# A Fourier-layer image tower on one core: the inverse x step moved whole behind the centre taps, in a hand-written order of matmuls

## The chip, the core and the metric

The kernel runs on one core of a Trainium2 chip. The metric is the device time of one execution in microseconds (us). Three runs of the kernel before took 1215.12, 1220.45 and 1225.88 us, median 1220.45.

A core has five engines with an instruction stream each: TensorE (PE; its weight loads are listed as PEld), VectorE (DVE), ScalarE (ACT), GpSimd (POOL) and SyncE (SP). Here SP and POOL issue the DMAs. Each engine runs its own stream in order; where one needs another's result it waits on a counting semaphore.

## The reference, cut to what matters

```python
h = concatenate([grid, x], -1) @ P_w + P_b              # 32 images, 64x64, 32 channels
for i in range(4):                                      # the four layers
    h_ft = rfft2(h)
    out_modes = einsum('bixy,ioxy->boxy', h_ft[:, :, :16, :16], spec_w[i])   # complex
    spec = irfft2(out_modes, s=(64, 64))
    conv = conv2d(h, conv_w[i], 3x3, 'SAME') + conv_b[i]
    h = leaky(spec + conv)
h = leaky(h @ Q1_w + Q1_b) @ Q2_w + Q2_b                # one channel: 32 x 64 x 64
h = h + attention(layernorm(h))                         # rows of an image are the tokens
h = h + mixture(layernorm(h))                           # causal attention, gates, small MLP
```

Only 16 x 16 Fourier modes are kept, so both transforms are matrix products with constant matrices. All data is fp32.

## The kernel before, in words

**Units.** The 32 images are worked in 16 pairs (`PAIRS`), four layers one after the other; T = 16 l + p counts pairs over all layers, `LAST` is p = 15. One pair's plane is 128 partitions by four *units* u of 512 values. Each unit has an accumulator of one PSUM bank, `acc[u]`.

**What is summed in an accumulator.** In layer 0 the first layer's convolution is folded into one product with `xcol` (`convolve_first`, one product per unit). In layers 1 to 3 the 3x3 convolution reads `halo`, a shifted copy of the plane in SBUF, in three kinds of products: `convolve_centre` (four 128x512 products, one per unit), `convolve_rows(T, v)` (v = 0 works on units 0 and 2, v = 1 on units 1 and 3; 16 products each) and `convolve_columns(T, v)` (8 each, same units). Onto the same accumulators `spectral(T, part)` adds the last step of the inverse transform, the inverse x step: 64 products of 64x64 in four parts of 16. ACT then reads the four accumulators (`evict`, one ACTIVATE each, bias and leaky) into `x_now`.

An fp32 product is recorded as two matmuls and two weight loads. In the profile's counts a pair has therefore 8 centre, 64 row, 32 column and 128 spectral matmuls.

**The transforms around it.** DVE transposes `x_now` (`turn_x`, two pieces, tile `xt`), PE does the rows of the forward transform (`rows_forward`, 16 matmuls by the profile's count), DVE transposes (`turn_rows`, tile `ft`), PE does the columns (`columns_forward`, 64), ACT copies the modes into `spec` (`spectrum`). At the layer's end `mix` multiplies all modes by the layer's weights `wspec` (256 matmuls in four quarters), and DVE turns each quarter (`turn_modes`, tile `zt`). For each pair `columns_back` (32) starts the inverse, DVE transposes (`turn_back`, tile `vt`), and `spectral` ends it. One part of `wspec` has to be negated on DVE before `mix` (`negate`). Between layers a pair's plane goes to HBM by a POOL DMA (`store`) and comes back as `halo` by 11 SP DMAs (`load_halo`).

**What sets the order.** Everything is written out by hand. For PE a pair is one function: `first_pair` (layer 0), `pair` (layers 1 and 2), `last_pair` (layer 3, with the head of pair p-1 and pieces of the later attention, `fronts`, between); `boundary` is the first pair of layers 1 to 3. DVE's loop over T is: `turn_rows(T+1)`, `turn_back(T+1)`, `turn_x(T+2)`, and for p = 8 `negate(l+1)`. ACT's loop over T is four `evict`, then `spectrum(T-1)`. PSUM is full: four accumulators, two banks for the forward transform, two for the inverse. So a unit's next centre product waits until ACT has read that accumulator (`s_x`), and `rows_forward(n)` waits for `turn_x(n)`, which waits for all four evictions of pair n-2.

## Time and profile before

| | us |
|---|---|
| median of 3 runs | 1220.45 |
| the profiled execution | 1218.4 |
| its span, first to last instruction | 1216.6 |
| PE busy | 1069.0 (88%) |
| DVE busy | 612.0 (50%) |
| ACT busy | 456.5 (38%) |
| mean granted TensorE clock | 0.963 of full |

A span is what the hardware profiler saw between the first and the last instruction; the execution's own time is 1.8 us more. Idle before an instruction is named with what released it; "issue" means that the engine waited for nothing that the profile shows. The rows on which the prediction rests stand two sections below.

### The profile page before, as it was taken

What the parts mean: (1) busy time and instruction counts of PE and PEld (TensorE: products, weight loads), DVE (VectorE), ACT (ScalarE), POOL (GpSimd) and SP (SyncE); (2) the same over time, 40 slices, a digit from 0 to 9 for tenths busy, and PEclk for the clock granted to TensorE, in tenths of its full rate; (3) what the DMA queues carried; (4) which work ended last, traced back from release to release, by engine and by line L of the source; (5) the groups of instructions that cost most, each with busy time, mean ns of one, the idle gap of its engine ahead of it and who ended that gap; (6) DMA issues with size and microseconds to landing.
All of it is one profiled execution on the core that took longest, in us unless ns stands there. A gap on an engine that the chain in (4) does not pass through costs nothing.

```text
span 1216.6 us, 47905 instructions
## 1 busy us (share of the span) xinstructions
PE 1069.0 (88%) x22416; PEld 565.3 (46%) x22416; DVE 612.0 (50%) x548; ACT 456.5 (38%) x889; POOL 83.7 (7%) x154
## 2 busy tenths in 40 slices
PE   4688888789989999889999899888999999899965
PEld 2445545454444444554444444533343444366722
DVE  3777787545555754455556554510221423277743
ACT  1245445313333332223333333223344443566523
POOL 2000000000000000000000000001212112110000
PEclk9899989899999999999999999999999999899986
DMA  9364445666776766686776767478545544000000
GB/s 312 143 209 135 133 135 165 200 218 192 210 223 201 225 210 195 197 283 213 217 212 208 219 205 212 134 182 201 139 115 141 145 121 108 5 6 1 2 1 17
DMA packets 50805, 194.25 MB, mean 160 GB/s; under 512 B 14928, under 2 KB 15696, under 8 KB 41040
## 3 DMA queue, kind: packets, MB, share of 16 engines
q1 hardware_dynamic: 40624, 138.23, 41.2%
q0 software_dynamic: 9984, 52.97, 12.0%
q8 instruction: 176, 2.88, 1.0%
q14 instruction: 21, 0.17, 0.0%
HBM read 138.19 MB, written 52.95 MB: 157 GB/s over the span
## 4 chain that ended last, share of the span: by engine, by line
PE 74%; DVE 8%; issue 8%; ACT 4%; DMA 1%; SPq 0%; DVEq 0%; ACTq 0%
PE psum L593 14%; PE psum L607 13%; PE psum L636 11%; PE psum L620 6%; PE psum L566 5%; PE psum L514 4%; PE psum L501 4%; PE psum L551 3%; ACT x_now L1017 3%; PE psum L654 3%; DVE xt L1195 2%; PE psum L838 2%; PE psum L578 1%; DMA halo<-activations 1%; PE psum L662 1%
## 5 line engine op out<-in xcount | busy, mean ns | idle before, releaser
L1017 ACT ACTIVATE x_now<-psum,conv_bias 128x512 f32<-128x512 f32 x256 | 157.4, 689 | 514.3 <-PE psum L636 497.2
L1195 DVE STREAM_TRANSPOSE xt<-x_now 128x1024 f32<-128x1024 f32 x100 | 204.5, 2082 | 116.4 <-ACT x_now L1017 110.5
L1225 DVE STREAM_TRANSPOSE vt<-psum 128x1024 f32<-128x1024 f32 x64 | 125.4, 1960 | 197.5 <-PE psum L566 197.5
L593 PE MATMUL psum<-halo,conv 128*128 128x512 f32 x384 | 184.8, 623 | 2.2 <-ACT x_now L1017 1.8
L607 PE MATMUL psum<-halo,conv 64*32 64x512 f32 x3072 | 177.7, 592 | 0.4 <-issue 0.4
L1202 DVE STREAM_TRANSPOSE ft<-psum 128x1024 f32<-128x1024 f32 x50 | 100.4, 2009 | 151.6 <-PE psum L501 151.5
L636 PE MATMUL psum<-dft,vt 64*64 64x64 f32 x8192 | 147.9, 222 | 27.7 <-issue 26.9
L636 PEld LDWEIGHTS psum<-dft,vt 64*64 64x64 f32 x8192 | 133.4, 136 | 72.6 <-issue 59.5
L325 ACT ACTIVATE spec<-psum 32x128 f32<-32x128 f32 x372 | 142.7, 384 | 40.3 <-PE psum L514 36.3
L593 PEld LDWEIGHTS psum<-halo,conv 128*128 128x128 f32 x384 | 71.3, 197 | 87.3 <-issue 61.2
L607 PEld LDWEIGHTS psum<-halo,conv 64*32 64x32 f32 x3072 | 53.4, 106 | 116.0 <-issue 115.8
L514 PE MATMUL psum<-dft,ft 128*32 128x64 f32 x3200 | 65.0, 232 | 35.8 <-issue 27.7
L620 PE MATMUL psum<-halo,conv 64*32 64x512 f32 x1536 | 93.6, 591 | 0.0
L566 PE MATMUL psum<-zt,dft 64*32 64x256 f32 x2048 | 82.0, 379 | 2.7 <-DVE vt L1225 1.4
L445 POOL DMA_DIRECT2D activations<-x_now x48 | 25.7, 535 | 726.5 <-ACT x_now L1017 726.5
L514 PEld LDWEIGHTS psum<-dft,ft 128*32 128x32 f32 x3200 | 53.4, 117 | 46.8 <-issue 29.2
L566 PEld LDWEIGHTS psum<-zt,dft 64*32 64x32 f32 x2048 | 50.7, 106 | 47.9 <-issue 37.4
L501 PE MATMUL psum<-xt,dft 64*32 64x512 f32 x800 | 55.6, 612 | 17.5 <-DVE xt L1195 17.5
L578 PE MATMUL psum<-xcol,conv 96*128 96x512 f32 x128 | 64.2, 647 | 0.0
L1024 ACT ACTIVATE xt<-psum,q1b 128x512 f32<-128x512 f32 x64 | 40.4, 683 | 44.2 <-PE psum L654 44.0
L620 PEld LDWEIGHTS psum<-halo,conv 64*32 64x32 f32 x1536 | 29.6, 106 | 54.7 <-issue 50.2
L452 POOL DMA_DIRECT2D tower_out<-ft x64 | 31.8, 503 | 245.6 <-ACT ft L1031 229.8
(150 smaller groups left out, 783.0 us busy)
## 6 DMA issues: line engine op xcount, KB each, us to landing
activations<-x_now POOLq DMA_DIRECT2D x48, 1056.0 KB, 7.2
halo<-activations SPq DMA_DIRECT2D x384, 132.0 KB, 4.7
halo<-activations SPq DMA_DIRECT2D x48, 528.0 KB, 5.7
halo<-activations SPq DMA_DIRECT2D x96, 264.0 KB, 6.3
wspec<-in_spec SPq DMA_DIRECT2D x16, 1024.0 KB, 10.1
xcol<-in_xcol SPq DMA_DIRECT2D x16, 384.0 KB, 4.4
x_now<-in_ser SPq DMA_DIRECT2D x2, 1056.0 KB, 6.9
spec<-in_onehot SPq DMA_DIRECT2D x1, 2048.0 KB, 17.7
```

Source lines behind the costliest of these rows:

```text
L325: return copy(spec[g:g + 32, 64 * qh:64 * qh + 64, ql, 2 * p:2 * p + 2].rearrange("p (y x) b -> p y b x", x=MODES), columned(X + 2)[32 * q ...
L501: z = mm(rowed[g:g + 32, f, :], ex[64 * f:64 * f + 64, :], xt[64 * f:64 * f + 64, at:at + 16, :], start=True, stop=True)
L514: z = mm(columned(n)[g:g + 32, 64 * kyb:64 * kyb + 64], ft[:, k0, :], ey[:, ri, :], start=(ri == 0), stop=(ri == 1))
L566: z = mm(backed[g:g + 32, cg, 256 * ri:256 * ri + 256], iy[64 * cg:64 * cg + 64, m, 32 * h:32 * h + 32], zt[64 * cg:64 * cg + 64, :, 2 * p ...
L593: mm(acc[u], centre[l - 1][:, u // 2, :], window(T, 0, None, u, 0, 0), start=True, stop=False, skip_group_check=True)
L607: z = mm(acc[u][g:g + 32, :], weight[64 * f:64 * f + 64, s, :], window(T, 0, f, u, di, dj), start=False, stop=False, skip_group_check=True)
L620: mm(acc[u][g:g + 32, :], edge_x[l - 1][64 * f:64 * f + 64, h, r, :], window(T, 1, f, u, 0, -1 if s == 0 else 1), start=False, stop=False, ...
L636: z = mm(acc[u][64 * s:64 * s + 64, at:at + 64], vt[64 * il:64 * il + 64, k, 4 * u + ih].rearrange("p r o -> p (r o)"), ix[64 * il:64 * il ...
L1017: copy(x_now[:, k, 16 * u:16 * u + 16, 0:G], acc[u].rearrange("p (i j) -> p i j", j=G), ACT.Prelu, bias=conv_bias[:, l:l + 1], alpha=SLOPE ...
L1195: vec.transpose(xt[:, 32 * m:32 * m + 32, :], x_now[:, n % 2, :, 0:G].rearrange("p (i m) j -> p m j i", m=2)[:, m]).then_inc(s_xt, 1)
L1202: vec.transpose(ft[:].rearrange("p k c -> p c k"), rowed.rearrange("p a b -> p (a b)").rearrange("p (i c) -> p c i", c=C)).then_inc(s_ft, 1)
L1225: vec.transpose(vt[:, k].rearrange("p h r o -> p (h r) o").rearrange("p y o -> p o y"), backed.rearrange("p a b -> p (a b)").rearrange("p ...
```

## The change

1. In layers 1 to 3 `spectral` moves from the end of a pair to right behind the four centre products, all four parts; the row and column products follow, and the column products now end a unit. Units 0 and 2 are then complete before 1 and 3, so centres and evictions go in the order 0, 2, 1, 3 (`units`, `evicted`). In `pair` the forward rows stand between the two halves of the row products. The first pair of a layer keeps its spectral step at the end.
2. In layer 0 a pair was: convolution, `rows_forward(T+1)`, `columns_back(T+1)`, `spectral(T)`, `columns_forward(T+1)`. It is now: two convolution products, `columns_forward(T)`, the other two, `spectral(T)`, `rows_forward(T+1)`, `columns_back(T+1)`. ACT's `spectrum` of layer 0 moves ahead of the evictions.
3. `negate` is cut from 4 instructions into 8 (`NEGATED`), the four quarters of `mix` wait for two each. In layer 0's own start it stands behind the copies of the modes; for the next layer one piece stands in each of the pairs 8 to 15.
4. The 4 MB of the next layer's weights, which SP issued in one go behind `mix`, go in four pieces with the pairs 2 to 5. The two masks of layer 3 (2 MB each), issued behind the halo of pair 3, go in four pieces with the pairs 3 to 6.
5. At the start PE waits for `dft` alone (`s_dft`), and the folding of weights stands behind the first forward rows. ACT's `head_read` stands behind all four evictions.

The places in PE's stream, first a pair of layer 1 (T = 17) and the head of the next, before. L593 is `convolve_centre`, L607 the row products, L501 `rows_forward`, L620 the column products, L566 `columns_back`, L636 `spectral`, L514 `columns_forward`; here a row counts fp32 products, half of the profile's matmuls:

```order
L593 MATMUL psum<-halo,conv 128x512 x4
L607 MATMUL psum<-halo,conv 32x512 x32
L501 MATMUL psum<-xt,dft 32x512 x8
L620 MATMUL psum<-halo,conv 32x512 x16
L566 MATMUL psum<-zt,dft 32x256 x16
L636 MATMUL psum<-dft,vt 64x64 x64
L514 MATMUL psum<-dft,ft 32x64 x32
```

And a pair of layer 1 (T = 18) with the change, where all these lines are 12 to 15 higher (L606 centre, L651 spectral, L620 rows, L513 forward rows, L633 columns, L578 back, L526 forward columns):

```order
L606 MATMUL psum<-halo,conv 128x512 x4
L651 MATMUL psum<-dft,vt 64x64 x64
L620 MATMUL psum<-halo,conv 32x512 x16
L513 MATMUL psum<-xt,dft 32x512 x8
L620 MATMUL psum<-halo,conv 32x512 x16
L633 MATMUL psum<-halo,conv 32x512 x16
L578 MATMUL psum<-zt,dft 32x256 x16
L526 MATMUL psum<-dft,ft 32x64 x32
```

The three rows of small products (16, 64 and 32) stood next to each other and are now in two places, 64 behind the centres and 48 at the end.

A pair of layer 0 on PE before (L578 is `convolve_first`):

```order
L578 MATMUL psum<-xcol,conv 128x512 x4
L501 MATMUL psum<-xt,dft 32x512 x8
L566 MATMUL psum<-zt,dft 32x256 x16
L636 MATMUL psum<-dft,vt 64x64 x64
L514 MATMUL psum<-dft,ft 32x64 x32
```

and with the change (L591 is `convolve_first`):

```order
L591 MATMUL psum<-xcol,conv 128x512 x2
L526 MATMUL psum<-dft,ft 32x64 x32
L591 MATMUL psum<-xcol,conv 128x512 x2
L651 MATMUL psum<-dft,vt 64x64 x64
L513 MATMUL psum<-xt,dft 32x512 x8
L578 MATMUL psum<-zt,dft 32x256 x16
```

`rows_forward` stood ahead of the pair's own `spectral` and stands behind it now.

DVE ahead of layer 0's `mix` before (L1212 is `negate`, L1315 the copies of the modes):

```order
L1195 STREAM_TRANSPOSE xt<-x_now 128x1024 x2
L1202 STREAM_TRANSPOSE ft<-psum 128x32x32
L1212 TENSOR_SCALAR wspec<-wspec 32x64x32 x4
L1315 COPY spec<-psum 64x4x64 x16
L1218 STREAM_TRANSPOSE zt<-psum 128x1024 x4
```

and with the change (L1240, L1342):

```order
L1223 STREAM_TRANSPOSE xt<-x_now 128x1024 x2
L1230 STREAM_TRANSPOSE ft<-psum 128x32x32
L1342 COPY spec<-psum 64x4x64 x16
L1240 TENSOR_SCALAR wspec<-wspec 32x8x4x32 x8
L1246 STREAM_TRANSPOSE zt<-psum 128x1024 x4
```

The negation, now in 8 pieces of half the size, stands behind the copies.

The diff, cut to its core:

```diff
-        NEGATED = 4
+        NEGATED = 8
+        def units(T):
+            return (0, 1, 2, 3) if T < PAIRS else (0, 2, 1, 3)
+        def evicted(T, u):
+            return 4 * T + units(T).index(u) + 1
...
-                    load_weights(l + 1)
                 for p in range(2, PAIRS):
                     T = l * PAIRS + p
+                    if l < NL - 1 and p < 6:
+                        load_weights(l + 1, p - 2)
...
-                    if l == NL - 1 and p == 3:
+                    if l == NL - 1 and 3 <= p < 7:
+                        b = slice(8 * (p - 3), 8 * (p - 3) + 8)
                         sp.wait_ge(s_mix, 4 * NL)
-                        sp.dma_start(lq[64:128]..., onehot_d).then_inc(t_mask, 16)
-                        sp.dma_start(kr[64:128]..., causal_d).then_inc(t_mask, 16)
+                        sp.dma_start(lq[64:128, b]..., onehot_d[:, b]).then_inc(t_mask, 16)
+                        sp.dma_start(kr[64:128, b]..., causal_d[:, b]).then_inc(t_mask, 16)
...
             def mix(l):
-                pe.wait_ge(s_neg, NEGATED * (l + 1))
...
                 for c in range(4):
+                    pe.wait_ge(s_neg, NEGATED * l + 2 * c + 2)
...
             def first_pair(p):
                 T = p
-                if p > 0:
-                    for u in range(4):
-                        convolve_first(T, u)
-                    rows_forward(T + 1)
-                if p < LAST:
+                for i in range(4):
+                    if p > 0:
+                        convolve_first(T, i)
+                    if p > 1 and i == 1:
+                        columns_forward(T)
+                if p == 0:
                     columns_back(T + 1)
                 for part in range(4):
                     spectral(T, part)
                 if p > 0:
-                    columns_forward(T + 1)
+                    rows_forward(T + 1)
+                if 0 < p < LAST:
+                    columns_back(T + 1)
             def pair(l, p):
...
+                for u in units(T):
+                    convolve_centre(T, u)
+                for part in range(4):
+                    spectral(T, part)
+                convolve_rows(T, 0)
+                rows_forward(T + 1)
+                convolve_rows(T, 1)
+                convolve_columns(T, 0)
+                convolve_columns(T, 1)
                 if p < LAST:
                     columns_back(T + 1)
-                for part in range(4):
-                    spectral(T, part)
-                if p > 0:
-                    columns_forward(T + 1)
+                columns_forward(T + 1)
...
-            pe.wait_ge(s_const, 16 * 4)
-            fold_weights()
+            pe.wait_ge(s_dft, 16)
             rows_forward(0)
+            pe.wait_ge(s_const, 16 * 3)
+            fold_weights()
...
-                evict(T, 0)
+                if l == 0 and p > 1:
+                    spectrum(T - 2)
+                for u in units(T):
+                    evict(T, u)
                 if last and p > 0:
                     head_read(p - 1)
-                for u in range(1, 4):
-                    evict(T, u)
...
-            negate(0)
             for n in range(1, 2 * SERIES, 2):
...                                                          # the copies of the modes
+            negate(0, *range(NEGATED))
...
-                        if p == PAIRS // 2:
-                            negate(l + 1)
+                        if p >= PAIRS - NEGATED:
+                            negate(l + 1, p - (PAIRS - NEGATED))
```

`last_pair` and `boundary` change in the same manner: `spectral` right behind the centres, and in layer 1's `boundary` the `columns_forward(T)` that layer 0 no longer has done.

## Rows read from the trace of the kernel before

**Rows 1.** The page: busy times, DMA queues (packets, MB, share), the chain by engine.
```profile
PE 1069.0 (88%) x22416; PEld 565.3 (46%) x22416; DVE 612.0 (50%) x548; ACT 456.5 (38%) x889; POOL 83.7 (7%) x154
...
q8 instruction: 176, 2.88, 1.0%
...
PE 74%; DVE 8%; issue 8%; ACT 4%; DMA 1%; SPq 0%; DVEq 0%; ACTq 0%
```

**Rows 2.** Windows of PE: from:to, length, busy (matmuls), granted clock, DMA share, GB/s.
```profile
74.50:148.40 73.90, 63.59 (x1751) 1.00 0.45 143
148.40:173.40 25.00, 21.05 (x515) 0.86 0.38 121
173.40:228.00 54.60, 45.13 (x1221) 0.97 0.67 202
228.00:260.40 32.40, 26.00 (x703) 0.95 0.37 134
260.40:281.00 20.60, 15.18 (x289) 0.91 0.75 232
281.00:496.80 215.80, 201.52 (x4798) 0.98 0.71 214
541.30:756.60 215.30, 200.17 (x4784) 0.99 0.72 214
801.70:843.50 41.80, 35.43 (x616) 0.92 0.94 208
843.50:859.60 16.10, 15.75 (x320) 0.98 0.55 139
843.50:1050.20 206.70, 205.47 (x3814) 1.00 0.47 121
```

**Rows 3.** Timeline of layer 0: start, us, what; in brackets idle before and releaser.
```profile
128.21 3.70 PE L578 MATMUL psum<-xcol,conv 96*128 96x512 f32 x8
...
129.29 4.08 DVE L1195 STREAM_TRANSPOSE xt<-x_now 128x1024 f32<-128x1024 f32 x2 [1.21 <-ACT x_now L1017]
...
133.42 1.09 PE L501 MATMUL psum<-xt,dft 64*32 64x512 f32 x16 [1.51 <-DVE xt L1195]
...
134.62 1.99 DVE L1202 STREAM_TRANSPOSE ft<-psum 128x1024 f32<-128x1024 f32 x1 [1.25 <-PE psum L501]
...
135.51 2.35 PE L636 MATMUL psum<-dft,vt 64*64 64x64 f32 x128
136.47 1.95 DVE L1225 STREAM_TRANSPOSE vt<-psum 128x1024 f32<-128x1024 f32 x1
137.40 2.42 ACT L1017 ACTIVATE x_now<-psum,conv_bias 128x512 f32<-128x512 f32 x4 [5.15 <-PE psum L636]
```

**Rows 4.** Timeline of layer 0, middle: the negation of the next weights.
```profile
154.98 4.97 DVE L1212 TENSOR_SCALAR wspec<-wspec 32x2048 f32<-32x2048 f32 x4
```

**Rows 5.** Timeline of the start, before the first pair.
```profile
9.07 2.02 PE L521 MATMUL psum<-fold_w,fold_p 128*96 128x128 f32 x8 [9.07 <-DMA proj<-in_proj]
...
30.52 4.97 DVE L1212 TENSOR_SCALAR wspec<-wspec 32x2048 f32<-32x2048 f32 x4 [7.66 <-DMA wspec<-in_spec]
...
36.76 7.76 PE L534 MATMUL psum<-series,proj 128*32 128x256 f32 x88 [7.61 <-DVE spec L1315]
...
46.49 7.68 PE L551 MATMUL psum<-spec,wspec 128*64 128x64 f32 x256 [1.97 <-ACT spec L1083]
...
55.52 1.13 PE L566 MATMUL psum<-zt,dft 64*32 64x256 f32 x32 [1.34 <-DVE zt L1218]
```

**Rows 6.** Windows of PE in layer 1: a pair without idle; one stall to the next.
```profile
314.40:328.35 13.95, 13.95 (x346) 1.00 0.63 203
359.44:376.07 16.63, 15.00 (x382) 1.00 0.67 202
```

**Rows 7.** Timeline of PE at the second of these stalls.
```profile
371.18 2.36 PE L636 MATMUL psum<-dft,vt 64*64 64x64 f32 x128
...
376.08 0.41 PE L514 MATMUL psum<-dft,ft 128*32 128x64 f32 x11 [1.63 <-issue]
```

More of the change, by code:

```diff
@@ L763, in last_pair @@
                 if p > 0:
-                    for u in range(4):
+                    for u in units(T):
                         convolve_centre(T, u)
+                    for part in range(4):
+                        spectral(T, part)
                     fronts(p, 0)
@@ L777, in last_pair @@
                     columns_back(T + 1)
-                for part in range(4):
-                    spectral(T, part)
-                    if p > 0 and part == 1:
-                        head_out(p - 1)
+                if p == 0:
+                    for part in range(4):
+                        spectral(T, part)
+                else:
+                    head_out(p - 1)
                 fronts(p, 2)
@@ L786, in boundary @@
                 T = l * PAIRS
-                for u in range(4):
+                for i, u in enumerate(units(T - 1)):
                     convolve_centre(T, u)
+                    if l == 1 and i == 1:
+                        columns_forward(T)
                 rows_forward(T + 1)
```

69 lines of the change are left out of this document (36 added, 33 removed).

## The prediction, made before the change was run

> **What bounds the kernel now.** I read the page first. PE is busy for 88% of the span and carries 74% of the chain that ended last, but 8% of that chain is "issue": PE waits and nothing shows why [rows 1]. Then I cut PE's time at each pair's first eviction and looked at windows [rows 2]; the cuts are evictions of T = 1, 8, 10, 15, 16, 17, 31, then 33, 47, 49, 51, 52 and 63.
>
> *Layer 0* takes (73.90 + 25.00 + 54.60) / 14 = 10.96 us a pair, and PE is idle in 10 of 74 us [rows 2]. The timeline shows the loop [rows 3]: `turn_x` 4.08 us on DVE ends at 133.37, the forward rows start at 133.42, `columns_back` and `spectral` follow, the eviction starts at 137.40, takes 2.42, and the next `turn_x` starts behind it. From `turn_x` at 129.29 that is 4.08 + 0.05 + 3.98 + 2.42 = 10.5 us. The eviction of pair T waits for the forward rows of T+1 only because they stand ahead of `spectral(T)` on PE.
>
> *Layers 1 and 2* take 215.80 / 14 and 215.30 / 14, or 15.4 us a pair, while a pair without idle takes 13.95 [rows 2, 6]. 1.43 us a pair are lost. The loss has a period. From one unexplained stall to the next PE issues 382 matmuls [rows 6], three times 127. A matmul comes with a weight load, and the instruction queue moved 2.88 MB in 176 packets for 2 x 22416 such records [rows 1], 255 for a packet. So PE stops at the edges of instruction blocks that have not arrived. The block behind the second stall starts at 376.08. The one before it began 127 matmuls earlier, 54 into the burst of 128 at 371.18 [rows 7], so at 372.0. The time from a block's begin to the next block's readiness, L, was 4.0 us there. A block that runs shorter than L ends in a stall. `columns_back`, `spectral` and `columns_forward` are 224 matmuls in some 4.2 us (128 of them in 2.36 with their tail [rows 7]), so a block that lies in them runs about 2 us. Averaged over where a block's edge may fall in the pair's 344 matmuls (2.7 edges a pair), L = 3.9 gives 1.57 us a pair, L = 3.5 gives 1.16. The measured 1.43 is L of about 3.8.
>
> The Trainium skill ("Runtime: NRT & Kernel Launch", Instruction fetch mechanics) confirms blocks of 256 instructions, but says that PE buffers 2048 of them and that crossing an edge is mostly hidden. By that rule the stalls have another cause; its time stands among the rivals. The measured spacing of 382 and the 4.0 us speak against the second half of the rule.
>
> *Layer 3* runs without idle from 843.50 (205.47 busy of 206.70), but its two pairs at 801.70 take 41.80 us at a DMA share of 0.94, against 16.1 for the next pair [rows 2]: the two masks, 4 MB, stand in the DMA queues ahead of halos and instruction blocks.
>
> **The change part by part**
>
> *Start.* Now `negate` holds DVE from 30.52 to 35.5, because it waits for the weights, and PE waits 7.61 us until 36.76 for copies behind it [rows 5]. With the copies first, PE's products run through: the forward rows no longer stand behind the folding that waits for `proj` until 9.07 (1 us), so they begin at about 24.4, 11.9 us of products and the last copy end at 37.1. The pieces: four instructions on 2048 elements took 4.97, so half of 1.24 each is the nearest price, 5.0 for eight; the other bound is 1.24 each, 9.9, if the shorter runs lose the speed. `turn_modes` stands behind all eight on DVE, so the third quarter of `mix` waits until 43.4; two quarters of `mix` of 1.92 (7.68 in all) and a transpose put `columns_back` at 49.0 instead of 55.52 [rows 5]. **-6.5** (bounds -2 and -8).
>
> *First two pairs.* From 55.52 to 74.50 are 19.0 us. The new order needs 1.1 + 3.7 + 1.1 + 2.0 to end the first spectral step, then 3.7 + 1.5 to the second's third part, 13.1, and I leave 0.9 for a late block: **-5.0**.
>
> *The pairs of layer 0.* With the forward rows behind `spectral`, the eviction leaves the loop. What remains is DVE's own round with one PE step in it: 4.08 + 1.25 (idle of DVE across the forward rows) + 1.99 + 1.95 = 9.27, with wake-ups 9.4 [rows 3]. PE needs 3.64 + 1.03 + 2.02 + 0.86 + 1.10 = 8.65, so 0.75 us of stalls is covered; I take 9.5. The single negation pushed the columns and the pair at 148.40 to 25.00 for two [rows 2] (the four stand at 154.98 [rows 4]); a piece of 0.62 ends within the 1.25 in which DVE waits anyway, cost nothing (a piece of 1.24 just fits too). Fourteen pairs: 153.5 becomes 14 x 9.5 = 133, and 3 for the burst of the first two halos that makes blocks late today: **-17.5**. `spectrum(T-2)` (about 3.1) ahead of the evictions has 3.3 us between its columns and the eviction, so it fits with little to spare. The boundary, 32.40, loses part of its late blocks: **-2**.
>
> *Layers 1 and 2.* Work stays 13.95. The 128 spectral matmuls lie between centres (8 in 3.7 us) and rows (32 in 1.8), the other 96 end the pair. Averaged again: L = 3.5 gives 0.25, 3.9 gives 0.40, 4.3 gives 0.6, 5 gives 1.15 us a pair. But the critical block now starts 2 to 6 us behind the completed accumulators, when the halo loads and the store have just begun; its L is longer than today's. I take 0.7. One wait is added: `convolve_columns` waits for the completion of the row products (`s_seg`), and the forward rows that stood between now stand in their middle. No row shows that wait; it is at least 0, and at most the 0.59 of a last matmul. The nearest is the wake-up of 0.1 behind PE plus the 0.15 by which the last one outlives its slot: 0.25. Per pair 1.43 becomes 0.95; 28 pairs: **-13.4**. The pair behind layer 1's boundary takes 20.60 at a granted clock of 0.91 with the 4 MB of weights in flight [rows 2]; with no weights there I leave 2 of its excess of 7.5: **-5.5**. The weight pieces are issued behind a halo and ahead of the wait for the next, into a DMA share of 0.7; hidden, if the halos keep arriving in the 16 us between their accumulators' completion and their centre. `turn_back` is ready 2.6 us before `spectral` wants it, evictions end under `columns_back` and `columns_forward`, `turn_x` has 2.3 us to spare. Boundaries: **-1**.
>
> *Layer 3.* Masks in pieces: 41.80 becomes 2 x 16.1: **-9.5**. The spectral matmuls, now split by `head_out`, become one burst of 128; with little DMA I take L = 3.5 and 0.17 us a pair: **+2.5**. The last pair's eviction starts with less work behind it: **-1**.
>
> The clock: each of the slow windows in [rows 2] (0.86, 0.91, 0.92, against 1.00) follows a stall, at 1.2 instead of 2.4 GHz; its price is in the terms above.
>
> Sum: -6.5 - 5.0 - 17.5 - 2 - 13.4 - 5.5 - 1 - 9.5 + 2.5 - 1 = -58.9. From the profiled execution's 1218.4 that is 1159.5; the median is 2 us above that execution, so I say **1160**.
>
> **The rivals**
>
> *A. The stalls only move* (17%). The late blocks depend on the count, not on the order, or L in the halo burst is near 5.3, where the average is again 1.43. Layers 1 and 2 then pay the new wait alone: +7 instead of -13.4, and layer 3 +5: **1183**. For it: today's pairs end their block stalls at the first matmul behind any dense stretch, and a dense stretch of 128 stays. Against: the stretch was 224 long, and a pair with no such edge in it runs through [rows 6]. By the Trainium skill's page on the runtime the edges cost next to nothing and this rival is the likely one.
>
> *B. Layer 0 keeps its period* (8%). DVE, ACT's `spectrum` or a block holds the eviction back and a pair stays near 10.4, less only the negation: 13 us of gain are gone, **1173**.
>
> *C. Blocks arrive in time throughout* (10%): L of 3.5 or less, 0.25 a pair, no visible wait: 28 x 0.7 = 20 more, **1140**.
>
> *D. The critical block leaves in the middle of the halo burst* (4%): the spectral step sits where 2 MB of halo and 1 MB of store fill the queues. At L = 7 the average is 5.0 us a pair, 28 x (5.0 + 0.25 - 1.43) = +107, and with -31 from layer 0 and -8 from layer 3 the time is **about 1286**. It decides the sign from L of 6.0, where the average is 2.6 a pair and 28 x (2.6 + 0.25 - 1.43) = 40 eats what the other terms gain. For it: the 20.60 with DMA share 0.75 [rows 2]. Against: the average DMA share stays at 0.7.
>
> The forecast itself has 61%, with 1145 to 1175 by L between 3.5 and 4.7 and by the start's bounds. The range is 1138 to 1190; it takes in A and C and leaves out D and both tails. A measurement of this kernel tells about 1% (12 us) from no change. Faster by over 1%: 0.91; within 1%: 0.05; slower: 0.04, which is D.
>
> **What the profile will show.** Evictions 9.4 to 9.6 us apart in layer 0, and PE idle ahead of the forward rows with DVE's `turn_x` as releaser. `columns_back` first at 49. Layers 1 and 2 at 14.9 a pair, "issue" halved, what remains of it inside `spectral` or the first rows, and gaps of 0.2 to 0.3 us ahead of the column products. No pair of layer 3 above 18.6. Wrong would be: layers 1 and 2 at 15.4 or more (A), evictions at 10.4 (B), or waits of PE for `vt`, `halo` or an eviction in every pair, which my slacks exclude.

## The result

| | median, us | lowest to highest | runs | ratio to before (95%) |
|---|---|---|---|---|
| the change | 1211.13 | 1197.40 to 1229.26 | 5 | 0.986 (0.982 to 0.990) |
| before, beside it | 1221.32 | 1215.12 to 1225.88 | 5 | |
| the change again, other session | 1208.53 | 1194.73 to 1222.69 | 6 | 0.988 (0.983 to 0.994) |
| before, beside it | 1217.60 | 1211.58 to 1223.57 | 17 | |

The change is 1.2 to 1.4% faster by these ratios and 0.8% by the medians (10.2 and 9.1 us): the ratios leave out slow executions, those over 1.5% above the fastest of the same kernel. The forecast was 1160, with 1138 to 1190 as its range: the sign was right, the size wrong by 51 us. The profile shown below is of the second session, an execution of 1208.76 us with a span of 1206.9. Executions of the changed kernel differ by 28 to 32 us within a session, and every figure for a stretch or a pair below comes from one execution of its kernel; a difference of a few us between two of them can be chance.

### The profile page after: what moved, and what is told of

Read it like the earlier page. It is cut to its first block, busy times and chain, and to the rows that moved or that the text cites. A ratio compares the mean times of both kernels' runs of the same rounds, so it can differ in the third digit from the quotient of the medians.

```text
span 1227.5 us, 47936 instructions
## 1 busy us (share of the span) xinstructions
PE 1092.3 (89%) x22416; PEld 558.1 (45%) x22416; DVE 608.9 (50%) x564; ACT 460.9 (38%) x889; POOL 84.2 (7%) x154
## 4 chain that ended last, share of the span: by engine, by line
PE 80%; issue 8%; DVE 7%; ACT 3%; DMA 1%; SPq 1%; DVEq 0%; ACTq 0%
PE psum L620 15%; PE psum L606 13%; PE psum L651 10%; PE psum L633 7%; PE psum L578 6%; PE psum L591 5%; PE psum L513 4%; PE psum L526 4%; PE psum L669 3%; PE psum L563 2%; PE psum L865 2%; PE psum L677 1%; DVE xt L1223 1%; DVE ft L1230 1%; DVE spec L1342 1%
## 5 line engine op out<-in xcount | busy, mean ns | idle before, releaser
L620 PE MATMUL psum<-halo,conv 64*32 64x512 f32 x3072 | 215.3, 615 | 23.7 <-issue 23.7
L606 PE MATMUL psum<-halo,conv 128*128 128x512 f32 x384 | 178.0, 605 | 3.9 <-DMA halo<-activations 3.2
L651 PEld LDWEIGHTS psum<-dft,vt 64*64 64x64 f32 x8192 | 126.4, 135 | 53.9 <-issue 53.9
L651 PE MATMUL psum<-dft,vt 64*64 64x64 f32 x8192 | 135.9, 220 | 5.9 <-issue 5.9
L620 PEld LDWEIGHTS psum<-halo,conv 64*32 64x32 f32 x3072 | 61.0, 108 | 134.7 <-issue 131.1
L606 PEld LDWEIGHTS psum<-halo,conv 128*128 128x128 f32 x384 | 68.5, 188 | 86.7 <-issue 78.1
L633 PE MATMUL psum<-halo,conv 64*32 64x512 f32 x1536 | 100.7, 610 | 4.9 <-issue 1.8
L578 PE MATMUL psum<-zt,dft 64*32 64x256 f32 x2048 | 88.2, 383 | 10.1 <-issue 7.4
L513 PE MATMUL psum<-xt,dft 64*32 64x512 f32 x800 | 67.4, 630 | 27.2 <-DVE xt L1223 15.1
L578 PEld LDWEIGHTS psum<-zt,dft 64*32 64x32 f32 x2048 | 54.6, 107 | 51.6 <-issue 43.0
L591 PE MATMUL psum<-xcol,conv 96*128 96x512 f32 x128 | 66.1, 643 | 0.4 <-ACT x_now L1044 0.4
L526 PEld LDWEIGHTS psum<-dft,ft 128*32 128x32 f32 x3200 | 49.0, 113 | 36.3 <-issue 25.6
L526 PE MATMUL psum<-dft,ft 128*32 128x64 f32 x3200 | 57.6, 225 | 5.9 <-DVE ft L1230 3.6
L633 PEld LDWEIGHTS psum<-halo,conv 64*32 64x32 f32 x1536 | 26.5, 108 | 77.8 <-issue 41.7
## 6 DMA issues: line engine op xcount, KB each, us to landing
wspec<-in_spec SPq DMA_DIRECT2D x16, 1024.0 KB, 10.3
```

The costliest lines, as they stand in the source:

```text
L513: z = mm(rowed[g:g + 32, f, :], ex[64 * f:64 * f + 64, :], xt[64 * f:64 * f + 64, at:at + 16, :], start=True, stop=True)
L526: z = mm(columned(n)[g:g + 32, 64 * kyb:64 * kyb + 64], ft[:, k0, :], ey[:, ri, :], start=(ri == 0), stop=(ri == 1))
L578: z = mm(backed[g:g + 32, cg, 256 * ri:256 * ri + 256], iy[64 * cg:64 * cg + 64, m, 32 * h:32 * h + 32], zt[64 * cg:64 * cg + 64, :, 2 * p ...
L591: mm(acc[u], conv0[:, u // 2, :], xcol[0:96, k, HALF * u:HALF * u + HALF], start=True, stop=False, skip_group_check=True)
L606: mm(acc[u], centre[l - 1][:, u // 2, :], window(T, 0, None, u, 0, 0), start=True, stop=False, skip_group_check=True)
L620: z = mm(acc[u][g:g + 32, :], weight[64 * f:64 * f + 64, s, :], window(T, 0, f, u, di, dj), start=False, stop=False, skip_group_check=True)
```

## The profile after

The page of the changed kernel, the lines that answer to [rows 1]:

```profile
PE 1082.1 (90%) x22416; PEld 554.1 (46%) x22416; DVE 609.8 (51%) x564; ACT 460.7 (38%) x889; POOL 84.0 (7%) x154
...
q8 instruction: 176, 2.88, 1.0%
...
PE 80%; issue 8%; DVE 7%; ACT 3%; DMA 1%; SPq 1%; DVEq 0%; ACTq 0%
...
L620 PE MATMUL psum<-halo,conv 64*32 64x512 f32 x3072 | 210.2, 605 | 26.1 <-issue 26.1
```

"issue" still is 8% of the chain, and 26.1 us of it now stand ahead of the row products (L620), the products right behind the spectral burst. Before, they stood ahead of the spectral step (26.9 us) and the forward columns (27.7).

Windows of PE at the cuts of [rows 2], with the same columns: evictions of T = 1, 8, 10, 15, 16, 17, 31, then 33 to 47, then 49, 51 and 63:

```profile
62.80:132.40 69.60, 65.42 (x1756) 0.98 0.61 201
132.40:150.30 17.90, 17.90 (x509) 1.00 0.51 168
150.30:202.10 51.80, 48.47 (x1256) 0.97 0.73 212
202.10:232.80 30.70, 25.94 (x715) 1.00 0.26 87
232.80:245.80 13.00, 11.98 (x267) 1.00 0.79 230
245.80:470.60 224.80, 209.71 (x4824) 0.98 0.74 220
514.20:738.00 223.80, 208.00 (x4824) 1.00 0.73 218
782.00:820.90 38.90, 33.84 (x616) 0.96 0.71 169
820.90:1040.00 219.10, 211.86 (x3840) 0.99 0.49 124
```

Put beside [rows 2], each stretch as its length after less its length before:

| stretch | forecast | measured |
|---|---|---|
| start to the first cut (74.5 before, 62.8 now) | -11.5 | -11.7 |
| T 1 to 15 (153.5 before, 139.3 now) | -17.5 | -14.2 |
| 15 to 16 | -2 | -1.7 |
| 16 to 17 | -5.5 | -7.6 |
| layers 1 and 2, 28 pairs | -13.4 | **+17.5** |
| the boundaries 31 to 33, 47 to 49 | -1 | -2.0 |
| 49 to 51, the masks | -9.5 | **-2.9** |
| 51 to 63, layer 3 | +2.5 | **+12.4** |
| tail | -1 | +0.5 |
| sum | -58.9 | -9.7 |

-9.7 is the difference of the spans, 1206.9 less 1216.6. The first four rows came nearly as forecast, -35.2 for -36.5. The gain was lost in layers 1 to 3: one term is off by 31 us, two more by 7 and 10.

*The start*, timeline (it answers to [rows 5]):

```profile
24.33 10.73 PE L546 MATMUL psum<-series,proj 128*32 128x256 f32 x128 [0.56 <-ACT series L1013]
...
36.85 5.71 DVE L1240 TENSOR_SCALAR wspec<-wspec 32x1024 f32<-32x1024 f32 x8
...
38.40 5.42 PE L563 MATMUL psum<-spec,wspec 128*64 128x64 f32 x128 [3.34 <-DVE wspec L1240]
...
49.28 1.13 PE L578 MATMUL psum<-zt,dft 64*32 64x256 f32 x32 [1.34 <-DVE zt L1246]
...
56.77 2.42 ACT L1044 ACTIVATE x_now<-psum,conv_bias 128x512 f32<-128x512 f32 x4 [20.52 <-issue]
...
62.82 2.42 ACT L1044 ACTIVATE x_now<-psum,conv_bias 128x512 f32<-128x512 f32 x4 [3.63 <-PE psum L651]
...
178.28 2.42 ACT L1044 ACTIVATE x_now<-psum,conv_bias 128x512 f32<-128x512 f32 x4 [0.26 <-PE psum L651]
178.42 0.68 DVE L1240 TENSOR_SCALAR wspec<-wspec 32x1024 f32<-32x1024 f32 x1
178.62 1.09 PE L513 MATMUL psum<-xt,dft 64*32 64x512 f32 x16
...
183.58 4.09 DVE L1223 STREAM_TRANSPOSE xt<-x_now 128x1024 f32<-128x1024 f32 x2
```

In this and the later timelines a row gives start, length and what ran; the bracket has the idle time before it and what ended that. The products run without the 7.61 us wait, from 24.33 (forecast 24.4). A negation piece takes 5.71 / 8 = 0.71 us (forecast 0.62) and `columns_back` begins at 49.28 (forecast 49.0). The last four rows are *layer 0*: the forward rows (178.62) follow the spectral step at once, and DVE's next `turn_x` starts 5.3 us behind the eviction without any idle: DVE's own round is the loop. The spacing of first evictions is 9.0 or 9.1 in six of the pairs and 9.3 to 9.5 in four later ones. Three pairs with weight pieces, 10.1, 13.1 and 10.3, and one of 14.3 in the burst of the first halos make the mean 9.95 instead of 9.5.

*Layer 1*, a pair that loses most, timeline of PE with the halo issues of SP:

```profile
313.35 2.43 ACT L1044 ACTIVATE x_now<-psum,conv_bias 128x512 f32<-128x512 f32 x4 [8.17 <-PE psum L633]
...
314.29 2.28 SPq L394 DMA_DIRECT2D halo<-activations  x4
...
319.78 2.10 PE L651 MATMUL psum<-dft,vt 64*64 64x64 f32 x128
...
321.81 1.94 PE L620 MATMUL psum<-halo,conv 64*32 64x512 f32 x30
...
327.19 0.59 PE L620 MATMUL psum<-halo,conv 64*32 64x512 f32 x1 [3.44 <-issue]
...
328.80 3.68 PE L620 MATMUL psum<-halo,conv 64*32 64x512 f32 x25
...
333.71 2.43 ACT L1044 ACTIVATE x_now<-psum,conv_bias 128x512 f32<-128x512 f32 x4 [14.28 <-PE psum L633]
...
342.18 1.95 PE L620 MATMUL psum<-halo,conv 64*32 64x512 f32 x32
```

The halo loads go out at 314.29. The spectral burst is at 319.78, five and a half microseconds into them. PE stops behind the 30th row product. A block is 127 matmuls, so the one that ended there began 97 matmuls before the rows, 31 into the burst, at 320.3. Its successor was ready at 327.19: L, the time from a block's first matmul to the next block's readiness, was 6.9 us, where I had read 4.0 from [rows 7]. Behind the stop, 25 row products take 3.68 us where 32 take 1.95 in the next pair. The granted clock there, from a window of PE:

```profile
328.40:331.80 3.40, 3.40 (x34) 0.50 0.02 5
```

That is 1.2 instead of 2.4 GHz. In layers 1 and 2 of this execution the granted clock fell twice, behind the two longest stops (2.93 and 3.44 us), and in layer 3 once, behind one of 1.92 us. The pair takes 333.71 - 313.35 = 20.4 us, a pair without a stop 14.3.

## The experiments

All ratios are against the kernel before, run on the same chip in the same session. "A pair" is the mean spacing of first evictions in layers 1 / 2 of the profiled execution, which can be 10 us faster than its kernel's median. It was 15.4 / 15.4 before and is 16.1 / 16.0 with the change.

### 1. Which part gains and which loses

**old_order_123**: the change, with layers 1 to 3 in the order of before.

```diff
             def pair(l, p):
-                for u in units(T):
+                for u in range(4):
                     convolve_centre(T, u)
-                for part in range(4):
-                    spectral(T, part)
                 convolve_rows(T, 0)
-                rows_forward(T + 1)
                 convolve_rows(T, 1)
+                rows_forward(T + 1)
                 convolve_columns(T, 0)
                 convolve_columns(T, 1)
...
+                for part in range(4):
+                    spectral(T, part)
                 columns_forward(T + 1)
```

> The change without its first part: in layers 1 to 3 the spectral step, the order of units and of head_read are as before; start, layer 0, negation, weights and masks as in the change. Theory F (instruction blocks are late in the halo burst that now lies ahead of the spectral matmuls): layers 1 and 2 return to 15.4 us a pair, layer 3 to the time of before less the masks' 6 to 10; start and layer 0 keep their 23 to 30 us. Sum 1178 to 1190, ratio 0.965 to 0.975. Theory W (weights and masks in pieces disturb the pairs beside them, the order is innocent): layers 1 and 2 stay at 16 or more, 1200 to 1215. If the start and layer 0 had gained nothing durable: 1212 to 1220.

**only_order_123**: the kernel before, with nothing but the new order of layers 1 to 3 (the same lines, other way round).

> The kernel before with the first part of the change alone: the new order in layers 1 to 3 (units 0, 2, 1, 3), everything else as before. Theory F: 28 pairs at 16.4 instead of 15.4 and 10 in layer 3, 1240 to 1260 us, ratio 1.02 to 1.03. Theory W: no loss, 1210 to 1222. My sum on record for this part alone would be -13 to -16, 1205.

| | median, us | ratio (95%) | a pair |
|---|---|---|---|
| old_order_123 | 1197.90 | 0.982 (0.978 to 0.986) | 15.3 / 15.6 |
| only_order_123 | 1240.49 | 1.018 (1.014 to 1.022) | 15.5 / 15.6 |

Alone, the new order of layers 1 to 3 makes the kernel 1.8% slower; without it, the rest of the change is 1.8% faster. In its own profile, 17.2 us longer than that of the kernel before, only_order_123 loses little in layers 1 and 2 (15.5 a pair). Windows of PE, layer 1 and layer 3:

```profile
281.00:498.00 217.00, 205.89 (x4824) 1.00 0.72 213
849.80:1066.10 216.30, 210.76 (x3845) 0.99 0.46 116
```

Layers 1 and 2 together cost 3.7 us, layer 3 (T = 51 to 63) 9.6, the masks 3.7 (45.5 instead of 41.8) and the stretch from T = 15 to 16 3.2 (35.6 instead of 32.4); the pair behind layer 1's boundary gains 3.9. So the largest single part of what the order costs by itself lies in layer 3, where the mean DMA share is below one half. That the order costs in sum is shown both ways; how it divides over the layers differs from kernel to kernel.

### 2. Are the halo bytes what makes the blocks late?

**change_small_halos** and **before_small_halos**: the same two kernels, each halo load cut to 8 elements of a partition, with all loads, waits and instructions kept. Their convolutions then work on other data, so these two kernels serve for timing alone.

```diff
                     to, of = TOP + 2 * UNIT * h, 2 * UNIT * h
-                    n = 2 * UNIT
+                    n = 8
```

> The change with each halo load cut to 8 elements a partition (the halo buffers are filled with zeros once; the convolution of layers 1 to 3 then computes on other data). Same instructions on PE, same DMAs by count, almost no bytes. Theory F (blocks are late because of the halo traffic): layers 1 and 2 come to 14.3 to 14.7 us a pair. Rival O (order of products and the added wait): 16 or more a pair, as in the change.

> The kernel before with the same cut of its halo loads. Theory F: the latency falls from about 4 us to about 3, the loss per pair from 1.4 to 0.5 to 0.9 (the stretch of 224 small matmuls stays), so 14.5 to 14.9 a pair: the two orders come within 0.4 us of each other, and the change's is the better. Rival O: 15.4 as it is, or at least 1 us below the change's.

| | median, us | ratio (95%) | a pair |
|---|---|---|---|
| change_small_halos | 1135.61 | 0.930 (0.918 to 0.942) | 14.4 / 14.4 |
| before_small_halos | 1177.11 | 0.964 (0.951 to 0.977) | 14.5 / 14.5 |

Layer 1 of change_small_halos as one window of PE:

```profile
240.30:442.10 201.80, 200.20 (x4824) 1.00 0.26 94
```

and of before_small_halos, with PE's largest wait in the window below it:

```profile
269.90:472.50 202.60, 196.38 (x4800) 1.00 0.22 79
```

```profile
PE psum L517 <- issue: 6.2, 7, 1.2
```

The halo bytes cost the change 1208.53 - 1135.61 = 73 us and the kernel before 41. In layer 1 of the change no wait of PE is left over 0.2 us: 14.42 a pair is 0.1 more than the 14.3 of a pair without a stop. That the products still follow one another on the same accumulators, as in the change, speaks against the rival of these expectations by which their order was the loss. In layer 3 (T = 51 to 63), too, the loss goes with the bytes: change_small_halos takes 205.8 us, before_small_halos 206.8.

Without the halo bytes the change is 42 us faster than the kernel before, but not by its order in layers 1 to 3. Of the 41.0 us between the two spans 11.6 lie at the start, 12.8 in layer 0's pairs, 5.2 behind layer 1's boundary and 5.5 at the masks; layers 1 and 2 give 1.7 and layer 3 gives 1.0. The split does shorten the stops, as the forecast had it: PE's idle time in the windows of layers 1 and 2 is 3.5 us instead of 11.8. The other products take 6.6 us more (PE busy 400.0 for 393.4), which takes most of it back. So even in empty queues the new order of layers 1 to 3 is worth 3 us, and with the halo traffic it costs.

### 3. The blocks one by one

The trace has the start of each packet of the instruction queue and of each matmul. I laid the grid of blocks (127 matmuls) over the matmuls and took for each block in layers 1 and 2 the time from its first matmul to the next packet's start (the *delay*), and the time until the next block's first matmul, which is L where PE stood waiting. "Us lost" is idle time of PE at these edges. The old-order kernels are those of section 6, small stores those of section 4.

| kernel | blocks that ended in a stop | delay, us | L, us | blocks that ran under 5 us | us lost |
|---|---|---|---|---|---|
| before | 25 | 1.43 | 4.09 | 34 | 27.2 |
| the change | 17 | 3.07 | 5.80 | 22 | 29.8 |
| old order, weights at once | 20 | 1.18 | 3.73 | | 25.3 |
| old order, halos sooner | 14 | 1.02 | 3.66 | | 19.0 |
| old order, halos later | 30 | 1.61 | 4.21 | | 41.3 |
| the change, blocks asked for at 6 to 8 us | 21 in all | 3.0 | | | 25.9 |
| the same, small stores | 22 in all | 3.1 | | | 22.3 |
| the same, small halos | 22 in all | 0.9 | | | 0.1 |

The last three rows take all blocks, stopped or not, that began 6 to 8 us behind their pair's first eviction. What counts as a stop moves these figures by up to a quarter: with every idle gap over 0.15 us at an edge, the kernel before has 27 stops, L 3.9 and 29.5 us, the change 16, L 6.0 and 25.6 us. By this second count the two other kernels with the new order in layers 1 and 2 have fewer stops but nearly the same L: only_order_123 13, L 5.4 and 19.6 us, change_weights_at_once (section 6) 13, L 5.6 and 18.1 us.

Idle time is not the whole loss. PE's idle time in the windows of layers 1 and 2 is 30.9 us in the change and 29.4 before, its busy time 417.7 and 401.7. A row product is recorded as some 0.6 us long, although 32 of them pass in 1.95, so its end covers the first half microsecond of a stop behind it; a spectral product (0.22) covers less.

A block that PE waits for is ready 2.4 to 2.8 us after its packet starts, in each kernel. What changes is the delay. With the change there are fewer short blocks, as forecast (22 for 34), but 25.9 of its 29.8 us are lost in those that were asked for in the middle of the halo loads and wait 3.0 us for their packet. With small halos the same blocks wait 0.9.

### 4. Halo, or halo and store together

**change_small_stores** and **before_small_stores**: POOL's stores of layers 1 and 2 cut to 8 elements, halo loads whole.

```diff
-                pool.dma_start(x_d[X % PAIRS], x_now[:, X % 2]...
+                n = PLANE if X < PAIRS else 8
+                pool.dma_start(x_d[X % PAIRS][:, 0:n], x_now[:, X % 2]...[:, 0:n]
```

> The change with the stores of layers 1 and 2 (POOL, 1056 KB a pair) cut to 8 elements a partition; layer 0 stores in full, so the convolutions of layers 2 and 3 compute on old data. The halo loads are whole. In the change nearly all loss (25.9 of 29.8 us in layers 1 and 2) stands behind blocks requested 6 to 8 us after the pair's first eviction, the time in which the store and the halo loads overlap. If the overlap makes the queue: their wait falls from about 3 us to about 1.5, layers 1 and 2 to 14.4 to 15.0 us a pair, 1150 to 1175 us. If the halo loads alone do it: 15.6 to 16.3 a pair, 1190 to 1210.

> The same cut in the kernel before, whose dense stretch starts 10 us and more behind the eviction, when the store is over. Overlap theory: little gain, 15.0 to 15.4 a pair. Halo loads alone: 15.4.

Measured: change_small_stores 1207.33, ratio 0.989 (0.980 to 0.997), 16.0 / 15.8 a pair; before_small_stores 1199.91, ratio 0.982 (0.975 to 0.990), 14.5 / 14.8 a pair. Windows of PE in layer 1, first of change_small_stores:

```profile
246.30:470.20 223.90, 210.23 (x4824) 0.98 0.58 151
```

then of before_small_stores:

```profile
282.40:484.70 202.30, 196.88 (x4800) 1.00 0.59 153
```

The same bytes are gone from both (0.74 of the DMA engines' time down to 0.58, 0.71 down to 0.59). The change gains nothing, so for its block the halo burst alone is enough; the old order gains 0.8 a pair, which neither expectation had foreseen. Its dense stretch begins about 11 us behind the pair's first eviction, at the tail of the halo loads. Their packets end 13.4 to 15.1 us behind that eviction in most pairs of layer 1 before, and 11.2 to 13.0 with small stores. The mean DMA share, on which I had argued against rival D, tells nothing here: at 0.58 or 0.59 one kernel takes 16.0 a pair and the other 14.5. What tells is what lies in the queue when a block is asked for.

### 5. Moving the burst of small products

**spread**: the change, the spectral parts apart in layers 1 and 2.

```diff
+                for i, u in enumerate(units(T)):
                     convolve_centre(T, u)
-                for part in range(4):
-                    spectral(T, part)
+                    if i % 2:
+                        spectral(T, i // 2)
                 convolve_rows(T, 0)
+                spectral(T, 3)
                 rows_forward(T + 1)
+                spectral(T, 2)
```

> The change with the four parts of the spectral step of layers 1 and 2 spread over the pair: part 0 between the centres of units 0, 2 and of 1, 3, part 1 behind those, part 3 behind the first row products, part 2 behind the forward rows. Same instructions, no dense stretch over 96 matmuls. Theory F: a block of 127 matmuls then runs at least 3.9 us (2.0 in the change), so at a latency of 5 to 6 us the loss falls from some 2.4 to 0.6 to 2.2 us a pair: 15.2 to 15.8 a pair, 1175 to 1195 us, 10 to 25 below the change. Rival O (the loss comes from products on one accumulator following each other, spectral behind centre and rows behind spectral, and from the added wait): spread has more such neighbours and is as slow as the change or slower, 1205 to 1225.

**late_spectral**: spectral behind both halves of the rows and the forward rows, columns last (layers 1 and 2; layer 3 in the old order).

```diff
-                for part in range(4):
-                    spectral(T, part)
                 convolve_rows(T, 0)
-                rows_forward(T + 1)
                 convolve_rows(T, 1)
+                rows_forward(T + 1)
+                for part in range(4):
+                    spectral(T, part)
                 convolve_columns(T, 0)
```

> Layers 1 and 2 with the spectral step behind the forward rows and ahead of the column products (which still end a unit, order 0, 2, 1, 3); layer 3 in its old order; start, layer 0, weights and masks as in the change. The dense stretch is split 128 to 96 as in the change, but the 128 now start some 10 us behind the completed accumulators, when the halo burst is nearly over, and no wait is added ahead of the columns. Theory F (place in the burst counts): no-stall pair 14.0, loss 0.5 to 1.0, so 14.5 to 15.0 a pair against 15.4 with the old order: 1172 to 1190 us, below old_order_123. Rival S (any split stretch is as late as the change's 128, place does not matter): 15.8 to 16.4 a pair, 1205 to 1215. Rival O (order of products on one accumulator): as slow as the change.

Measured: spread 1215.65, ratio 0.997 (0.995 to 1.000), 16.2 / 16.0 a pair; late_spectral 1204.59, ratio 0.989 (0.984 to 0.993), 16.0 / 16.1 a pair. The group of the spectral matmuls on the page of spread:

```profile
L651 PE MATMUL psum<-dft,vt 64*64 64x64 f32 x8192 | 157.8, 222 | 11.6 <-issue 11.4
```

and of the change:

```profile
L651 PE MATMUL psum<-dft,vt 64*64 64x64 f32 x8192 | 135.8, 220 | 6.2 <-issue 6.2
```

Both miss their expectation (15.2 to 15.8 and 14.5 to 15.0 a pair). Spread loses only some 10 us to late blocks in layers 1 and 2, but its pair without any stop takes 15.3 instead of 14.3. The same 8192 matmuls, each as long as ever (222 against 220 ns), keep PE busy 22 us longer, as their runs are shorter and more. Spread adds six switches between tile shapes to a pair: 0.12 us for each by that busy time, 0.17 by the 1.0 us of the pair. It also adds places where products follow others on the same accumulator, the rival of its expectation; no run here separates the two. Late_spectral moves the burst some 6 us towards the end of the halo loads and gains nothing on the change in layers 1 and 2. By the second count of section 3, its stopped blocks have a delay of 2.3 and an L of 4.9 us, less than the change's, but 40 of its blocks run under 5 us instead of 22, and 31 us are lost for 26: the loads have not ended there either, and more blocks are exposed.

### 6. Moving the halo loads

**old_order_early_halos** and **late_spectral_early_halos**: the halos of pairs 16 and 17 are loaded during pairs 8 and 10 of layer 0, when their planes have long been stored, instead of in a burst at layer 0's end.

```diff
                         load_columns(p)
+                        if p in (8, 10):
+                            load_halo(PAIRS + (p - 8) // 2)
```

> old_order_123 with the halos of layer 1's first two pairs loaded at pairs 8 and 10 of layer 0 instead of together at its end. Theory F: the 16 us between the evictions of pairs 14 and 15, which held 9.1 without halo bytes, fall to 9.1 to 10.5, so 4 to 7 us less than old_order_123; a little of it comes back as later blocks in pairs 8 to 11. If the two late evictions have another cause: within 1 us of old_order_123.

> Both of the last two together. Theory F: the gains add, 1165 to 1185 us, the fastest of all so far and 2.5 to 4% under the kernel before. Rival S: 1200 to 1210.

Measured: 1201.75, ratio 0.985 (0.980 to 0.990), and 1214.77, ratio 0.996 (0.993 to 0.999), so 3.9 and 10.2 us slower than old_order_123 and late_spectral. A miss. The pair that ends layer 0's regular pairs (T = 14 to 15) does come down from 15.6 to 9.0, but those from T = 7 to 10 take 13.5, 11.6 and 14.7 instead of 9.5, 9.0 and 9.0: the burst costs where it is put, and more there. Layers 1 and 2 are slower as well, 15.8 / 15.8 and 16.3 / 16.3 a pair; why is open.

**old_order_weights_at_once**: old_order_123, with the next layer's weights in one go again.

```diff
+                    for q in range(4):
+                        load_weights(l + 1, q)
                 for p in range(2, PAIRS):
-                    if l < NL - 1 and p < 6:
-                        load_weights(l + 1, p - 2)
```

> old_order_123 with each layer's weights issued at once behind mix, as in the kernel before (masks stay in pieces). It prices the pieces. Theory F: 4 MB in one burst make one or two blocks very late (17.8 to 20.6 us for the first or second pair of a layer) and leave the others alone, the pieces put some 1 to 2 us on each of three or four pairs: within 5 us either way, the pair behind layer 1's boundary at 18 to 21 instead of 14.7 and layer 0's pairs 2 to 5 at 9 to 10 instead of 10 to 13.

**old_order_halos_sooner** and **old_order_halos_later**: from there, SP's wait ahead of the halo loads is moved: to the end of the column products, 3.1 us sooner, or to the end of the forward columns.

```diff
-                    sp.wait_ge(s_acc, 4 * (T - 2) + 4)
+                    sp.wait_ge(s_col, 4 * (T - 2 - PAIRS) + 4)     # sooner
...
                     sp.wait_ge(s_acc, 4 * (T - 2) + 4)
+                    sp.wait_ge(s_fy, T)                            # later
```

> old_order_weights_at_once (1187.25 us, 15.4 us a pair) with one wait of SP changed: a pair's halo loads start when the column products have read the buffer, and not behind the spectral step, so 3.1 us sooner, over columns_back and spectral. PE's, DVE's and ACT's streams are the same but for the signal. Theory F (a dense stretch under the halo burst has late blocks): the latency of the blocks in it goes from 3.9 to 5 or more, a pair to 15.9 to 16.6, 1200 to 1220 us. Rival S (PE's order alone decides, the moment of the loads does not): 1182 to 1192, 15.4 a pair.

> The same kernel with the wait moved the other way: halo loads start behind columns_forward as well, 1 us later than in the kernel before, over the centre and row products. Theory F: the last dense piece is free of the burst, 14.9 to 15.3 a pair, 1176 to 1187 us; if the loads then land too late for their centre, PE waits for halo and it is 1187 to 1200. Rival S: 1182 to 1192.

**change_weights_at_once**: the change with the same edit of the weights.

> The change with each layer's weights issued at once again: its order of PE in layers 1 to 3, without the pieces. If the two losses add: 1208.5 less the 10.6 that the pieces cost in the old order, 1194 to 1202, ratio 0.978 to 0.985, layer 0 at 9.3 a pair and the pair behind layer 1's boundary near 18. If the pieces cost only beside the old order: 1204 to 1212.

| | median, us | ratio (95%) | a pair |
|---|---|---|---|
| old_order_weights_at_once | 1187.25 | 0.973 (0.968 to 0.978) | 15.4 / 15.4 |
| old_order_halos_sooner | **1174.42** | 0.966 (0.963 to 0.970) | 15.0 / 15.3 |
| old_order_halos_later | 1199.46 | 0.987 (0.983 to 0.991) | 15.9 / 15.8 |
| change_weights_at_once | 1207.19 | 0.986 (0.981 to 0.990) | 15.4 / 15.7 |

PE's waits in layer 1 of old_order_halos_sooner (L652 is the spectral step, L527 the forward columns):

```profile
PE psum L527 <- issue: 8.5, 6, 2.0
PE psum L652 <- issue: 2.4, 2, 1.4
```

and of old_order_halos_later (L651 the spectral step):

```profile
PE psum L651 <- issue: 12.8, 8, 2.9
PE psum L528 <- issue: 7.7, 6, 1.4
```

Sooner gains 12.8 us on the kernel it was made from, later loses 12.2. I had expected the opposite sign, from the thought that a load behind the dense stretch lets its block pass. But a pair's loads last 13 to 14 us in most pairs, so a later start pushes their tail into the *next* pair's dense stretch. That stretch begins 11 us behind the first eviction. In most pairs of layer 1 the packets end 10.1 to 11.5 us behind it with the sooner start, 13.4 to 14.5 in the kernel it was made from, and 15.6 to 17.4 with the later start. The waits ahead of the spectral step in layer 1 are 2.4 us in the one and 12.8 in the other, those ahead of the forward columns hardly differ (8.5, 7.7). The profiled executions with the sooner start and of its origin are 7.8 us apart: 5.9 of it is in layer 1, 0.4 in layer 2 and 3.5 at the masks, whose halo loads start sooner too.

The weights in pieces, part 4 of the change, cost 10.6 us in the old order (1197.90 to 1187.25). The pair behind layer 1's boundary does get 4.6 us shorter by the pieces (14.7 for 19.3), but the pairs T = 1 to 14 take 9.73 instead of 9.26 each, 6 us, and each layer has pieces: the three pairs behind that one in layer 1 and their like in layer 2, beside which the pieces go out, take 103.4 us instead of 90.4. In the profiles of the change and change_weights_at_once those six pairs take 106.6 and 96.4. But by the medians the same edit moves the change by only 1.3 us, less than the two can be told apart by; the two effects do not simply add, and why stays open.

Old_order_halos_sooner is the fastest kernel of this study, 3.4% under before and, by the medians of two sessions, 34 us under the change (by the ratios some 27).

## Why the prediction was wrong

**The step that failed** is the size of L in "Layers 1 and 2": "its L is longer than today's. I take 0.7". The direction was seen and the size was not. The loss without the new wait is 16.06 - 14.3 = 1.76 us a pair in layer 1 and 1.69 in layer 2, not 0.7, because the L of the critical block is 5.8 (17 blocks), not 4.3 or so. The average holds roughly: it gave 1.43 at L = 5.3 and 2.6 at 6.0, with the measured 1.76 at 5.8 between them, and 0.25 at 3.5, where small halos measure 0.1. With 1.73 in place of 0.7, 28 x (1.73 + 0.3 - 1.43) = +17, as measured. This is rival D's mechanism at less than its price (4% was too little for it).

How much of the +17.5 is the order alone is less certain. In only_order_123 and change_weights_at_once, with the same order, L is 5.4 and 5.6, but the loss beyond 14.3 is 1.2 / 1.3 and 1.1 / 1.4 us a pair, and layers 1 and 2 cost 3.7 and 5.2 us more than before. The rest is seen only with weight pieces in the queues, and between single executions. All three kernels lie above the 0.7, and the order alone costs 23 us by the medians where this part was forecast to gain.

**A second term put at nothing** is the weights in pieces: "hidden, if the halos keep arriving". In the old order they cost 10.6 us, and the three pairs of layer 0 beside them take 10.1, 13.1 and 10.3 us instead of 9.5.

**Why 3.9 was the wrong row.** [Rows 7] gave the L of blocks that leave 10 to 16 us behind a pair's first eviction, at the tail of the halo loads (delay 1 to 2 us). The change moves the burst to where the block leaves 6 to 8 us behind it, in their middle. I argued against D with the DMA share of a whole pair, which cannot show it.

**The Trainium skill** ("Runtime: NRT & Kernel Launch", Instruction fetch mechanics) holds that the crossing of an instruction block is mostly hidden. The measured idle time of 27 to 30 us at block edges in 28 pairs is not hidden; with small halos next to none of it is left in the change, so there the rule does fit. Its block size of 256 instructions fits the grid of 127 matmuls with their loads.

**Layer 3** (+12.4 for +2.5). The same step: "with little DMA I take L = 3.5". The share is 0.49, yet PE now stops ahead of the row products for 4.3 us and ahead of `fronts` (L669) for 2.6; before there was no such stop. On the grid of section 3 five blocks end in a stop there, with L from 4.9 to 8.2 us. The other half is busy time (211.86 for 205.47 us), partly a lower clock behind one stop; I have not split it further. Old_order_123 has 17.40 a pair there, before 17.23, the change 18.26 and only_order_123 18.02, so the order causes it; with small halos the change has 17.15, so it does so through the halo traffic. Pairs reach 21.3 us, where the forecast had none above 18.6.

**The masks** (-9.5 for -2.9). Two things add up here. In pieces the masks do not leave the two pairs at 16.1 each: old_order_123 has 36.4 us for 41.8, a gain of 5.4, and its later pairs of the layer are 2.1 us longer than before. And the new order costs 3.7 us in these two pairs by itself (only_order_123, 45.5 for 41.8); from there to the change the pieces gain 6.6. My test for masks and weights alike was whether halos arrive in time; that a piece can delay an instruction block as well was left out. That this is how the pieces cost is the likely reading, and I have not traced it block by block.

**What held.** The start to 0.3 us; the order of layer 0 (9.0 to 9.5 a pair for 9.4, and 9.95 with the disturbed ones); the negation in pieces; the pair behind layer 1's boundary (-7.6 for -5.5), though the pieces that free it cost more in the pairs after it; the new wait of 0.25 a pair (a pair without stops is 14.3 for 13.95, 0.3). Old_order_123 is the change without its new order of layers 1 to 3, and it gains more than the whole.

**The chances.** 61% on my own L and 4% on D was too sure, for an L read in a place where the block would no longer leave. An L between 4.7, my range's end, and 6.0 had only rival A.

## What to carry to other kernels

In this kernel a stretch of short instructions drains a block of instructions faster than the next one arrives (127 matmuls in about 2 us, L of 3 to 7), and how fast it arrives depends on what is in the DMA queues at the moment the block is asked for. So read, before moving such a stretch, which transfers are under way in its new place, and move the transfers (here 3 us sooner, 13 us gained) rather than cut up the work, which cost a microsecond a pair. A mean DMA share over a pair tells nothing about it; an experiment with tiny transfers and everything else kept does, in one run. Large loads cut into pieces are not free either: the weights in pieces cost 10.6 us in the old order.

## What was not expected of the hardware

- The next block was ready 2.4 to 2.8 us after its instruction packet started, in every kernel. For blocks asked for 6 to 8 us behind the first eviction, the packet started 0.9 us after the current block's first matmul with small halos, and 3.0 on average with whole ones.
- Spreading 128 matmuls of 64x64 between those of other tile shapes cost 0.12 to 0.17 us for each change of shape, if the shape is the cause: 157.8 us busy for 135.8 on the same 8192 matmuls.
- A stop of 3.44 us at a block's edge was followed by 25 matmuls in 3.68 us at a granted clock of 0.50, so that the pair lost 6.1 us by one late block. One of 1.9 us, in layer 3 of the change, was followed by that clock as well.
